# The first chunk of a two-layer kernel is loaded in two halves, the shared weights are loaded ahead of chunk two, and all instruction orders are planned anew

## The chip, the core and the metric

The kernel runs on one core of one Trainium2 chip. The metric is the time of one execution on the device, in microseconds (us); lower is better. Beside each time stands one execution that the hardware profiler recorded; the views below are of that one. The engines are PE (TensorE), DVE (VectorE), ACT (ScalarE), POOL (GpSimd) and SP (SyncE, which here only issues transfers). PEld is PE's loading of stationary operands, which overlaps PE.

## What is computed

A sequence x of 16 batches of 256 rows of 128 features goes through two gated layers; everything is float32. Cut to what matters here:

```python
xn = layernorm(x)                       # 4096 rows of 128
f = xn @ W.T + b                        # layer 0, attention
a = softmax(f @ f.T + distance_bias) @ f      # per batch of 256 rows
shared = (silu(xn @ Gs.T) * (xn @ Us.T)) @ Ds.T          # inner width 256
probs = sigmoid(xn @ router.T + bias)                    # 8 experts
w = top-2 of probs, normalised
combined = sum over the 2 experts of w * ((silu(xn @ G[e].T) * (xn @ U[e].T)) @ D[e].T)
x = x + a * silu(shared + combined)

xn = layernorm(x)                       # layer 1
s = attention over 16 heads, linear in the rows: projection, squares, softmax over heads, output projection
expert of a batch = argmax of a small network on the batch's last row
g = xn + 0.3 * ((gelu(xn @ W1[e] + b1) @ W2[e] + b2) @ Wo + bo)
x = x + s * silu(g)
```

## The kernel before

The 4096 rows are 32 tiles of 128 rows, four to a **chunk** (chunks 0 to 7), two to a batch. There are no loops over engines' work at run time and no scheduler in the compiler's sense: each engine's program is a long list of calls written out by a planner, such as `gate(3, 0)` (step 3, PSUM bank 0), and each step waits on semaphores for what it needs. An engine works through its list strictly in order. So the list decides both what an engine does next and what it waits for next, and a step that waits holds up all that stands behind it on its engine. 71 products of one 128-row unit with one expert (**units** 0 to 70) stand in the middle of the kernel.

The stages, and the lines of the profile that belong to them:

- **Start.** SP issues the loads of x (`load_x`, 256 KB a chunk, L245), of the constants C in three parts (L249, the second part at L257, the third at L264), of WA (router and layer-0 projection, L251) and of WB (the shared expert's weights, L253). PE runs `warm`, products of ones into a bank that nobody reads (L461), until its first real work is there. DVE makes a chunk's moments (`stats0`, L1089 and L1092, waits for the chunk's load), ACT the root (`root0`, L1894), DVE the normalised chunk XA (`norm0`, L1097 and L1100).
- **Layer 0, dense part.** PE turns a chunk (`turn_in`, L474), ACT copies it out as XT (L1907). From XT, PE makes `features` (L484, evicted by DVE at L1119), `gate` (L510) and `up` (L516) of the shared expert, `down` (L524); `turn_f` (L501) turns the features for the scores. DVE's `upper()` (L1124) makes a bf16 copy of a triangle of ones from the second part of C, and waits for its load. `prob`, `best`, `second` (from L1162) choose the two experts of a row, `ranks` on PE (L494) counts, and `positions` on DVE (L1202 to L1222) gives each row its place in a scratch. This is done in two sets: set 0 is chunks 0 to 2, set 1 the rest.
- **Dispatch.** POOL scatters the rows of a tile with two indirect transfers (L2412), 24 transfers for set 0 and 40 for set 1. Meanwhile scores (L532), softmax and `mix` (L551) run.
- **Units.** SP fetches the 128 rows of a unit back from the scratch (`fetch`, L283), PE turns four units at once (`turn_x`, L566), `gate_up` (L580), ACT silu (L1961), DVE `hidden` (L1317), PE `down_e` (L588), ACT scales the result (YS, L1968, eight buffers) and POOL scatters it (`scat`, L2435). A fetch of unit u waits for the scatter of unit u-16. `collect` (L293) loads a chunk's results back, 512 KB each; `root1` (L1894) is the root of the second layernorm.
- **Layer 1.** For chunks 0 to 5 it is begun between the last units, and ends with `store` (L333).

ACT holds the tables of few functions at once: between a root and a silu stands an ACT_TABLE_LOAD.

Of the kernel before, what the change touches and what calls it, by code (L numbers as in the profile page):

```python
# [34 lines left out]
WARM = 32  # L35
# [35 lines left out]
def program(nc, D, out):  # L71
    with ExitStack() as ctx:
# [88 lines left out]
        d_x = [sem(f"d_x{c}") for c in range(8)]  # L161
        d_id, d_wa, d_c, d_di, d_fill, d_dist = (sem("d_" + n) for n in ("id", "wa", "c", "di", "fill", "dist"))
# [75 lines left out]
        ident = c_("ident")  # L238
# [4 lines left out]
        def _(e):  # L243
# [105 lines left out]
            fetch(5)  # L349
            ends()  # L350
            fetch(6)
# [19 lines left out]
            store_b()  # L371
            fetch(26)
            fetch(27)
            load_w2()
# [3 lines left out]
            fetch(31)  # L378
            fetch(32)
# [6 lines left out]
            fetch(39)  # L386
            fetch(40)
# [7 lines left out]
            collect(1)  # L395
            fetch(47)
            fetch(48)
            collect(2)
            fetch(49)
            fetch(50)  # L400
            fetch(51)
            fetch(52)
# [15 lines left out]
            fetch(68)  # L418
            collect(3)
            collect(4)  # L420
            collect(5)
            store_w2(0)
            fetch(69)
            fetch(70)
            store_w2(1)
# [17 lines left out]
            expert1(13)  # L443
            expert1(14)
            store(0)
            expert1(15)
            store(1)
# [9 lines left out]
        def _(e):  # L457
# [9 lines left out]

            def turn_in(c, k, free=None, n=0):
                e.wait_ge(s_xa, c + 1)
                if c == 0:  # L470
                    e.wait_ge(d_id, 16)
                when(free, n)
                for j in range(4):
                    m = e.transpose(PS[k][:, j * 128:(j + 1) * 128], XA[:, 4 * c + j, 0:128], ident)  # L474
                m.then_inc(p_xt, 1)

            def features(b, k, free=None, n=0):

                e.wait_ge(s_xt, b // 2 + 1)
# [24 lines left out]
            def gate(j, k, free=None, n=0):  # L504
                c, f = divmod(j, 2)
                e.wait_ge(s_xt, c + 1)
                if j == 0:
                    e.wait_ge(d_wb, 16)
                when(free, n)
# [189 lines left out]
            turn_in(0, 0)  # L699
            gate(0, 0)  # L700
            features(0, 6)
            gate(1, 2)
            features(1, 3)
            turn_in(1, 0, s_sg, 1)
            up(0, 5)
            features(2, 0)
            up(1, 1)
            features(3, 3, s_f, 2)
            turn_in(2, 2, s_sg, 2)
            turn_f(0, 4)  # L710
            gate(2, 7)
            features(4, 3, s_f, 4)
            features(5, 2)
            up(2, 6)
            gate(3, 0)
            gate(4, 5)
            turn_in(3, 1, s_hh, 2)
            up(3, 2)
            down(0, 4, s_ft, 1)
            features(6, 1)  # L720
            ranks(0, 7, s_sg, 3)
            gate(5, 3)
            up(4, 1, s_f, 7)
            gate(6, 5, s_sg, 5)
            gate(7, 0)
            up(5, 7, s_places, 1)
            down(1, 6)
            turn_in(4, 2)
            up(6, 1)
            gate(8, 5)  # L730
            turn_f(1, 3)
            turn_f(2, 2)
            features(7, 4)
            down(2, 7)
            up(7, 3, s_ft, 2)
            turn_in(5, 6)
            gate(9, 4, s_f, 8)
            features(8, 0)
            features(9, 6, s_xt, 6)
            turn_in(6, 5)  # L740
            features(10, 1, s_hh, 7)
            features(11, 2)
            features(12, 0, s_f, 9)
            gate(10, 7)
            turn_in(7, 2, s_f, 12)
            up(8, 4, s_sg, 10)
            features(13, 3)
# [335 lines left out]
        def _(e):  # L1083
# [19 lines left out]
            def stats0(c):  # L1103
                e.wait_ge(d_x[c], 16)
                moments(4 * c, 4, s_mv)
# [1513 lines left out]
```

## Time and profile before

| | us |
|---|---|
| median of 3 runs | 285.37 (283.64 to 285.94) |
| the profiled execution's own time | 284.54 |
| its span on the core | 282.7 |

The profiled execution's own time is 1.8 us over its span: that much lies around the part that the engines' records cover. The page of the profile gives busy time of each engine, the same in 40 slices, and the costliest groups; the timeline gives single instructions with the idle time of their engine just before them and what released it.

### The profile page before, as it was taken

The numbers are of one execution on the slowest core, as the hardware profiler recorded it, in microseconds if no ns is written. First come the engines' busy times: TensorE is split into PE (matmuls) and PEld (weight loads), VectorE is DVE, ScalarE is ACT, GpSimd is POOL, SyncE is SP. The second block draws the span as 40 slices with busy tenths as digits, with TensorE's granted clock in tenths as the row PEclk, the third lists the DMA queues.
The fourth block names the chain that finished last, engine by engine and source line by source line (L and its number), as shares of the span: only waits on it lengthen the run. The fifth ranks groups of instructions, "written<-read, shape, count | busy, mean of one in ns | idle before, by whom it ended". The sixth has DMA issues, their size and how long they took to land.

```text
span 282.7 us, 6870 instructions
## 1 busy us (share of the span) xinstructions
PE 267.5 (95%) x1982; PEld 231.1 (82%) x1982; DVE 220.4 (78%) x828; ACT 192.4 (68%) x443; POOL 155.5 (55%) x175
## 2 busy tenths in 40 slices
PE   8899999999999999999999899999998989989992
PEld 5566877667898999999899899999887668858892
DVE  4898987996668668545455579858989999998996
ACT  2876764434555586466455466869979989989882
POOL 3100777777777777777677563773644853121140
PEclk9999999999999999999999999999999999999999
DMA  6997111113562111236432742234613847501813
GB/s 194 313 401 257 47 51 57 49 57 85 144 147 65 47 59 56 78 114 218 132 95 77 255 140 67 76 96 150 210 56 106 183 150 225 135 20 46 264 65 114
DMA packets 31221, 36.03 MB, mean 127 GB/s; under 512 B 4792, under 2 KB 24386, under 8 KB 30928
## 3 DMA queue, kind: packets, MB, share of 16 engines
q1 hardware_dynamic: 26864, 27.13, 32.8%
q0 software_dynamic: 4320, 8.47, 8.9%
q8 instruction: 17, 0.28, 0.4%
q14 instruction: 20, 0.16, 0.2%
HBM read 22.97 MB, written 14.12 MB: 131 GB/s over the span
## 4 chain that ended last, share of the span: by engine, by line
PE 59%; DVE 13%; DMA 9%; issue 8%; POOL 4%; ACT 3%; SPq 2%; DVEq 1%; POOLq 0%; ACTq 0%
PE PS L580 13%; PE PS L588 7%; PE PS L551 5%; PE PS L524 5%; PE PS L532 5%; PE PS L516 5%; PE PS L510 4%; DMA yc_scratch<-YS,XS 3%; POOL yc_scratch L2435 2%; PE PS L484 2%; DMA DI<-in_dest 2%; PE PS L566 2%; DMA XB<-yc_scratch 2%; DMA XB<-wf_scratch 2%; PE PS L666 1%
## 5 line engine op out<-in xcount | busy, mean ns | idle before, releaser
L2435 POOL DMA_INDIRECT yc_scratch<-YS,XS x71 | 73.3, 1032 | 40.8 <-ACT YS L1968 25.5
L580 PE MATMUL PS<-XG,XT 128*128 128x128 f32 x568 | 71.8, 276 | 0.6 <-DVE HHE L1317 0.5
L580 PEld LDWEIGHTS PS<-XG,XT 128*128 128x128 f32 x568 | 67.3, 192 | 1.7 <-issue 1.4
L1317 DVE TENSOR_TENSOR HHE<-EP,PS 128x256 f32<-128x256 f32 x71 | 28.6, 415 | 25.0 <-ACT EP L1961 17.6
L2412 POOL DMA_INDIRECT xs_scratch<-XA,POS x32 | 31.8, 994 | 22.9 <-issue 22.9
L1961 ACT ACTIVATE EP<-PS 128x256 f32<-128x256 f32 x71 | 26.6, 388 | 24.4 <-PE PS L580 21.9
L588 PE MATMUL PS<-WE,HHE 128*128 x284 | 41.2, 279 | 1.2 <-DVE HHE L1317 1.0
L588 PEld LDWEIGHTS PS<-WE,HHE 128*128 128x128 f32 x284 | 36.2, 191 | 3.5 <-issue 3.3
L2412 POOL DMA_INDIRECT xs_scratch<-XB,POS x32 | 31.6, 989 | 9.8 <-issue 9.8
L1329 DVE COPY XT<-WE 128x512 f32 x71 | 29.9, 443 | 5.6 <-PE PS L580 5.3
L1968 ACT ACTIVATE YS<-PS,XS 128x128 f32<-128x128 f32 x71 | 25.3, 371 | 9.0 <-PE PS L588 8.4
L2421 POOL COPY XT<-C 128x256 f32<-128x256 f32 x16 | 5.9, 400 | 24.8 <-DVE C L1438 24.7
L1100 DVE TENSOR_SCALAR XA<-X,MV,RS 128x128 f32<-128x128 f32 x64 | 19.1, 375 | 0.6
L551 PE MATMUL PS<-F,EP 128*128 128x129 f32 x128 | 16.9, 277 | 0.6 <-ACT EP L1937 0.5
L510 PE MATMUL PS<-XT,WB 128*128 128x512 f32 x32 | 16.3, 601 | 0.9 <-DMA WB<-in_wb 0.9
L551 PEld LDWEIGHTS PS<-F,EP 128*128 128x128 f32 x128 | 15.6, 191 | 1.8 <-ACT EP L1937 0.9
L524 PEld LDWEIGHTS PS<-WB,EP 128*128 128x128 f32 x128 | 15.2, 192 | 1.9 <-issue 1.2
L1089 DVE BATCH_NORM_STATS2 ST<-X 128x6 f32<-128x128 f32 x64 | 13.8, 276 | 3.7 <-DMA X<-in_x 3.7
L532 PE MATMUL PS<-FT 128*128 128x256 f32 x64 | 16.2, 381 | 0.0
L516 PE MATMUL PS<-XT,WB 128*128 128x512 f32 x32 | 16.2, 593 | 0.0
L1298 DVE CUSTOM_DVE_ANT_0 EP<-PS,C 128x256 f32<-128x256 f32 x32 | 12.2, 420 | 5.0 <-ACT EP L1937 3.6
L1937 ACT ACTIVATE EP<-EP 128x512 f32<-128x512 f32 x16 | 10.0, 629 | 8.9 <-DVE EP L1306 5.0
(222 smaller groups left out, 562.1 us busy)
## 6 DMA issues: line engine op xcount, KB each, us to landing
XS<-xs_scratch SPq DMA_DIRECT2D x71, 65.0 KB
XB<-yc_scratch SPq DMA_DIRECT2D x8, 512.0 KB, 4.6
WE<-in_we SPq DMA_DIRECT2D x1, 3072.0 KB, 14.7
X<-in_x SPq DMA_DIRECT2D x8, 256.0 KB, 5.6
out<-X SPq DMA_DIRECT2D x8, 256.0 KB, 2.5
S<-wf_scratch SPq DMA_DIRECT2D x7, 257.0 KB, 3.8
XB<-wf_scratch SPq DMA_DIRECT2D x6, 257.0 KB, 4.0
yc_scratch<-YS,XS POOLq DMA_INDIRECT x71, 2.4
```

The source lines that it names most:

```text
L510: e.matmul(PS[k][:, :], WB[:, f * 128:(f + 1) * 128], tile(XT, 4 * c, 4), start=True, stop=True).then_inc(p_g, 1)
L516: e.matmul(PS[k][:, :], WB[:, 256 + f * 128:256 + (f + 1) * 128], tile(XT, 4 * c, 4), start=True, stop=True).then_inc(p_u, 1)
L524: m = e.matmul(PS[k][:, t * 128:(t + 1) * 128], HHS[:, (2 * c + f) % 3, t * 128:(t + 1) * 128], WB[:, 512 + f * 128:512 + (f + 1) * 128], ...
L532: m = e.matmul(PS[k][:, i * 256:(i + 1) * 256], tile(FT, 2 * b + i), tile(FT, 2 * b, 2), start=True, stop=True)
L551: m = e.matmul(PS[k][:, i * 129:(i + 1) * 129], PT[:, kb, j, i * 128:(i + 1) * 128], F[:, 2 * b + j, 0:129], start=j == 0, stop=j == 1)
L580: m = e.matmul(PS[k][:, f * 128:(f + 1) * 128], WC[:, u % 4, f * 128:(f + 1) * 128], XG[:, g % 2, j * 128:(j + 1) * 128], start=True, stop ...
L588: m = e.matmul(PS[k][:, 0:128], HHE[:, u % 3, f * 128:(f + 1) * 128], WE[:, bass.ds(reg[u // 4][u % 4] + (512 + f * 128), 128)], start=f = ...
L1317: e.tensor_tensor(HHE[:, u % 3, :], SGE[:, u % 3, :], PS[k][:, 256:512], ALU.mult).then_inc(s_hhe, 1)
L1329: e.tensor_copy(WC[:, u % 4, :], WE[:, bass.ds(reg[u // 4][u % 4], 512)]).then_inc(s_wc, 1)
L1961: e.activation(SGE[:, u % 3, :], PS[k][:, 0:256], ACT.Silu, bias=0.0, scale=1.0).then_inc(s_sge, 1)
L2412: e.indirect_dma_start(out=xs, out_offset=bass.IndirectOffsetOnAxis(ap=POS[:, s, t:t + 1], axis=0), in_=T[:, t, :], in_offset=None, bounds ...
L2435: e.indirect_dma_start(out=yc, out_offset=bass.IndirectOffsetOnAxis(ap=XS[:, g % 4, j, 128:129].bitcast(U32), axis=0), in_=YS[:, u % 8, :] ...
```

## The change

1. Chunk 0 is loaded, normalised, turned and copied in two halves of 128 KB (`load_half`, `stats_first`, `norm_first`, `turn_first`, `root_first`); the first product with WB goes in two halves too, so that its first half needs only the first half of the chunk. The semaphores of the following chunks count one more.
2. WB is issued as SP's fourth load, ahead of chunk 1, no longer behind chunk 2.
3. `warm` makes 18 products instead of 32.
4. The lists of PE, DVE, ACT, SP and POOL and the PSUM banks of all steps are planned anew.

```diff
-WARM = 32
+WARM = 18
...
-            load_x(0)
+            def load_half(b):
+                e.dma_start(X[:, 2 * b:2 * b + 2, :].rearrange("p i d -> p (i d)"),
+                            D["x"].rearrange("(c b) (p i) d -> c b p (i d)", b=2, i=2)[0, b]).then_inc(d_x[0] if b else d_xh, 16)
+
+            load_half(0)
             e.dma_start(C[:, 0:129], D["consts"][:, 0:129]).then_inc(d_id, 16)
+            load_half(1)
+            e.dma_start(WB[:, :], D["wb"]).then_inc(d_wb, 16)
             load_x(1)
             e.dma_start(WA[:, :], D["wa"]).then_inc(d_wa, 16)
             load_x(2)
-            e.dma_start(WB[:, :], D["wb"]).then_inc(d_wb, 16)
...
             def gate(j, k, free=None, n=0):
                 c, f = divmod(j, 2)
-                e.wait_ge(s_xt, c + 1)
                 if j == 0:
+                    e.wait_ge(s_xt, 1)
                     e.wait_ge(d_wb, 16)
+                    when(free, n)
+                    e.matmul(PS[k][:, 0:256], WB[:, 0:128], tile(XT, 0, 2), start=True, stop=True)
+                    e.wait_ge(s_xt, 2)
+                    e.matmul(PS[k][:, 256:512], WB[:, 0:128], tile(XT, 2, 2), start=True, stop=True).then_inc(p_g, 1)
+                    return
+                e.wait_ge(s_xt, c + 2)
...
+            def stats_first():
+                e.wait_ge(d_xh, 16)
+                moments(0, 2, s_mv)
+
+            def norm_first():
+                e.wait_ge(s_sd, 1)
+                normalize(0, 2, s_xa)
...
+            stats_first()
             stats0(0)
+            norm_first()
             norm0(0)
             stats0(1)
+            upper()
             stats0(2)
             norm0(1)
+            features(0, 1)
+            norm0(2)
```

The orders as built, at the three places that matter below. **DVE at the start, before**, from the end of chunk 2's moments (BN_AGGR) to the CAST of `upper()`; RECIPROCAL and TENSOR_SCALAR are a chunk's normalisation:

```order
L1092 BN_AGGR MV<-ST 128x2 x4
L1097 RECIPROCAL RS<-RS 128x4
L1100 TENSOR_SCALAR XA<-X,MV,RS 128x128 x4
L1128 COPY XA<-DI 128x32
L1129 COPY XB<-DI 128x32
L1119 TENSOR_TENSOR F<-PS,WA 128x274
L1089 BN_STATS ST<-X 128x6 x4
L1092 BN_AGGR MV<-ST 128x2 x4
L1119 TENSOR_TENSOR F<-PS,WA 128x274
L1097 RECIPROCAL RS<-RS 128x4
L1100 TENSOR_SCALAR XA<-X,MV,RS 128x128 x4
L1124 CAST BFC<-C 128x128
```

**DVE at the start, after**, from the moments of chunk 1, which stand behind both halves of chunk 0:

```order
L1108 BN_STATS ST<-X 128x6 x4
L1111 BN_AGGR MV<-ST 128x2 x4
L1151 CAST BFC<-C 128x128
L1108 BN_STATS ST<-X 128x6 x4
L1111 BN_AGGR MV<-ST 128x2 x4
L1116 RECIPROCAL RS<-RS 128x4
L1119 TENSOR_SCALAR XA<-X,MV,RS 128x128 x4
L1146 TENSOR_TENSOR F<-PS,WA 128x274
L1116 RECIPROCAL RS<-RS 128x4
L1119 TENSOR_SCALAR XA<-X,MV,RS 128x128 x4
L1146 TENSOR_TENSOR F<-PS,WA 128x274
L1155 COPY XA<-DI 128x32
```

The CAST of `upper()`, which waits for the second part of C, has moved from behind the normalisations of chunks 1 and 2 to a place ahead of the moments of chunk 2, and so ahead of both; the copies from DI have moved behind them.

**SP at the start, before**, where each row is one load:

```order
L245 DMA X<-in_x 128x2x256
L249 DMA C<-in_consts 128x129
L245 DMA X<-in_x 128x2x256
L251 DMA WA<-in_wa 128x274
L245 DMA X<-in_x 128x2x256
L253 DMA WB<-in_wb 128x768
L245 DMA X<-in_x 128x2x256 x2
L257 DMA C<-in_consts 128x258
L258 DMA DI<-in_dest 128x64
```

**SP at the start, after**:

```order
L250 DMA X<-in_x 128x256
L254 DMA C<-in_consts 128x129
L250 DMA X<-in_x 128x256
L256 DMA WB<-in_wb 128x768
L246 DMA X<-in_x 128x2x256
L258 DMA WA<-in_wa 128x274
L246 DMA X<-in_x 128x2x256 x3
L263 DMA C<-in_consts 128x258
```

The load of WB has moved ahead of those of chunk 1, WA and chunk 2. The bytes ahead of the second part of C (the 128x258 row) are the same as before.

**SP in the middle, before**, from the table load ahead of unit 44 (L283 is a fetch, L293 a collect; an ISA row sets up the fetch behind it):

```order
L231 TENSOR_LOAD EI
L283 ISA
L283 DMA XS<-xs_scratch 128x130
L293 DMA XB<-yc_scratch 128x2x512
L283 ISA
L283 DMA XS<-xs_scratch 128x130
L283 ISA
L283 DMA XS<-xs_scratch 128x130
L293 DMA XB<-yc_scratch 128x2x512
L283 ISA
L283 DMA XS<-xs_scratch 128x130
L231 TENSOR_LOAD EI
```

**SP in the middle, after**, at the same place:

```order
L232 TENSOR_LOAD EI
L289 ISA
L289 DMA XS<-xs_scratch 128x130
L299 DMA XB<-yc_scratch 128x2x512
L289 ISA
L289 DMA XS<-xs_scratch 128x130
L289 ISA
L289 DMA XS<-xs_scratch 128x130
L289 ISA
L289 DMA XS<-xs_scratch 128x130
L232 TENSOR_LOAD EI
L289 ISA
```

The collect of chunk 0 still stands behind the fetch of unit 44, but that of chunk 1 no longer stands between the fetches of units 46 and 47; it and the next come behind unit 51.

Two more moves, read off the lists by hand: the `turn_x` of units 28 to 31 stands behind 1.8 us more of PE's work than before, and that of units 44 to 47 behind 1.3 us more (each step counted at the time that its products took before); and on ACT `root1` of chunks 0, 1 and 2 stands in one run between one pair of ACT_TABLE_LOADs, where chunk 2 had its own pair before. ACT has 33 such loads where it had 35.

## Rows read from the trace of the kernel before

**Rows 1.** The page: busy time of all engines, then PE, DVE and POOL in 40 slices (tenths).

```profile
PE 267.5 (95%) x1982; PEld 231.1 (82%) x1982; DVE 220.4 (78%) x828; ACT 192.4 (68%) x443; POOL 155.5 (55%) x175
...
PE   8899999999999999999999899999998989989992
```

**Rows 2.** Windows: stretch, its length, busy (and instructions) of PE, PEld, DVE, ACT, POOL, clock, DMA.

```profile
2.00:6.00 4.00, 4.00 (x21) 2.82 (x20) 2.09 (x12) 0.53 (x3) 0.40 (x2) 1.00 0.85 265
6.20:7.00 0.80, 0.80 (x9) 0.72 (x8) 0.80 (x5) 0.00 (x0) 0.49 (x1) 1.00 1.10 294
28.00:40.00 12.00, 12.00 (x83) 9.66 (x82) 11.79 (x54) 9.09 (x17) 9.26 (x10) 1.00 0.15 50
140.00:180.00 40.00, 38.19 (x327) 36.85 (x327) 27.10 (x78) 24.21 (x62) 24.58 (x24) 1.00 0.40 120
180.00:220.00 40.00, 38.06 (x324) 35.22 (x324) 33.21 (x122) 34.89 (x87) 22.48 (x22) 1.00 0.39 124
220.00:240.00 20.00, 18.92 (x132) 14.22 (x132) 18.95 (x82) 18.91 (x47) 11.16 (x16) 1.00 0.66 180
```

**Rows 3.** Timeline of the first 14 us: start, length, engine, line, tiles, count, idle before.

```profile
1.32 6.02 PE L461 MATMUL PS<-BFC 128*128 128x256 bf16 x32 [1.32 <-POOL ONE L2386]
...
3.51 0.87 DVE L1089 BATCH_NORM_STATS2 ST<-X 128x6 f32<-128x128 f32 x4 [3.51 <-DMA X<-in_x]
...
4.72 0.47 SPq L257 DMA_DIRECT2D C<-in_consts  x1
...
7.18 0.60 PE L474 MATMUL PS<-C,XA 128*128 128x128 f32 x4
...
7.63 0.87 DVE L1089 BATCH_NORM_STATS2 ST<-X 128x6 f32<-128x128 f32 x4 [0.22 <-DMA X<-in_x]
...
8.69 1.10 PE L510 MATMUL PS<-XT,WB 128*128 128x512 f32 x2 [0.90 <-DMA WB<-in_wb]
...
8.88 1.11 DVE L1100 TENSOR_SCALAR XA<-X,MV,RS 128x128 f32<-128x128 f32 x4
...
11.41 0.60 PE L474 MATMUL PS<-C,XA 128*128 128x128 f32 x4
...
13.67 0.22 DVE L1124 CAST BFC<-C 128x128 bf16<-128x128 f32 x1
```

**Rows 4.** DMA issues of the first 16 us: KB each, median us from issue to landing.

```profile
WB<-in_wb SPq DMA_DIRECT2D x1, 384.0 KB, 5.3
...
C<-in_consts SPq DMA_DIRECT2D x1, 129.0 KB, 5.6
```

**Rows 5.** Timeline of DVE: `best(0)` begins, and `positions(0)` begins.

```profile
18.91 0.31 DVE L1162 TENSOR_REDUCE RW<-XS 128x12 f32<-128x96 f32 x1
...
24.44 0.34 DVE L1202 TENSOR_TENSOR_SCAN XS<-ONE,PS 128x96 f32<-128x96 f32 x1
```

**Rows 6.** Timeline of POOL: the first dispatch, and the end of its unbroken work.

```profile
27.88 1.15 POOL L2412 DMA_INDIRECT xs_scratch<-XA,POS  x1 [13.45 <-issue]
...
141.51 0.97 POOL L2435 DMA_INDIRECT yc_scratch<-YS,XS  x1 [0.88 <-ACT YS L1968]
```

**Rows 7.** Timeline of PE, 120 to 215 us: three of the rows with idle time.

```profile
137.43 0.66 PE L566 MATMUL PS<-C,XS 128*128 128x128 f32 x4 [0.54 <-DMA XS<-xs_scratch]
...
161.19 0.66 PE L566 MATMUL PS<-C,XS 128*128 128x128 f32 x4 [0.92 <-DMA XS<-xs_scratch]
...
199.19 1.16 PE L688 MATMUL PS<-WD,XA 128*128 128x128 f32 x8 [0.51 <-DVE HHE L1317]
```

**Rows 8.** Timeline of SP's queue around the first collects.

```profile
156.32 0.43 SPq L293 DMA_DIRECT2D XB<-yc_scratch  x1
156.99 2.65 SPq L283 DMA_DIRECT2D XS<-xs_scratch  x2
```

**Rows 9.** Timeline of ACT around the root of chunk 2 in layer 1.

```profile
190.91 1.28 ACT L1894 ACT_TABLE_LOAD   x1
...
193.26 1.28 ACT L1961 ACT_TABLE_LOAD   x1
```

More of the change, by code:

```diff
@@ new lines, in _ @@
+            features(3, 7)
+            turn_f(0, 6)
+            features(4, 4, s_f, 3)
+            features(5, 0)
+            gate(3, 1, s_hh, 2)
+            turn_f(1, 0, s_f, 6)
+            down(0, 7)
+            turn_in(3, 4)
+            up(2, 5)
+            turn_f(2, 3, s_sg, 3)
+            gate(4, 2)
+            up(3, 0, s_ft, 2)
+            features(6, 4)
+            ranks(0, 2, s_sg, 5)
+            up(4, 1)
+            gate(5, 7, s_sh, 1)
+            features(7, 6)
+            up(5, 5, s_hh, 3)
@@ new lines, in _ @@
+            gate(6, 7, s_sg, 6)
+            gate(7, 0, s_hh, 4)
+            down(1, 3)
+            up(6, 6, s_f, 8)
+            up(7, 7, s_sg, 7)
+            turn_in(4, 3, s_sh, 2)
+            turn_f(3, 1)
+            down(2, 0, s_sg, 8)
+            gate(8, 5)
+            up(8, 1, s_ft, 4)
+            gate(9, 6, s_hh, 7)
+            features(8, 3)
+            turn_in(5, 4)
+            features(9, 5, s_sg, 9)
+            up(9, 7)
+            turn_in(6, 3, s_f, 9)
+            features(10, 4)
@@ L2217, in _ @@
-            gate(42, 2)
-            down_e(39, 0)
-            fuse(0, 5)
-            down_e(40, 3)
+            down_e(29, 0)
+            down_e(30, 2)
+            gate(31, 1)
+            gate(32, 6)
+            gate(33, 4)
+            turn_x(9, 7)
+            down_e(31, 0)
+            down_e(32, 7)
+            gate(34, 2)
+            gate(35, 4)
+            down_e(33, 0)
+            gate(36, 1)
+            gate(37, 7)
+            down_e(34, 5)
+            down_e(35, 6)
+            gate(38, 4)
@@ new lines, in _ @@
+            turn_x(10, 3)
+            gate(39, 7)
+            down_e(36, 4)
+            down_e(37, 0)
+            down_e(38, 7)
+            gate(40, 6)
+            turn_x(11, 4)
+            gate(41, 1)
+            gate(42, 2)
+            down_e(39, 1)
+            gate(43, 0)
+            down_e(40, 4)
+            gated(0)
+            down_e(41, 1)
+            turn_x(12, 4)
+            down_e(42, 7)
+            down_e(43, 1)
+            gate(44, 6)
+            gate(45, 0)
+            gate(46, 7)
@@ L2272, in _ @@
+            gate(58, 5)
+            turn1(1, 6)
+            down_e(55, 0)
+            keep(0, 4)
+            squares(1, 0)
+            down_e(56, 2)
+            turn1(2, 6)
+            gate(59, 7)
+            keep(1, 0)
+            gate(60, 5)
             down_e(57, 4)
@@ L2291, in _ @@
+            heads(0, 5)
+            turn_x(16, 1)
+            squares(2, 3)
+            gate(63, 0)
+            down_e(59, 2)
+            keep(2, 3)
+            down_e(60, 6)
+            gated(4)
+            gate(64, 1)
+            down_e(61, 0)
+            fuse(2, 5)
+            fuse(3, 6)
+            gate(65, 7)
+            gated(5)
+            turn_x(17, 3)
+            gate(66, 4)
+            down_e(62, 0)
             sel_exp(0)
-            down_e(62, 4)
             down_e(63, 0)
-            fuse(2, 3)
```

1680 lines of the change are left out of this document (803 added, 877 removed).

## The prediction

> **What bounds the kernel now.** I read the page's busy times first: PE is busy 267.5 us of a 282.7 us span, DVE 78%, ACT 68%, POOL 55% [rows 1]. The slices show where PE is not full: the first two, and the last third. The windows say the same in us [rows 2]. From 28 to 40 PE has no idle time at all and DVE hardly any (11.79 of 12.00), and PE's slices stay full from there to the last third. From 140 to 220 PE idles 3.75 us in short waits, and from 220 on DVE and ACT are as full as PE (18.95 and 18.91 of 20). So a microsecond lost or won ahead of 28 us has nothing behind it that soaks it up until about 137 us; and behind 220 us the end is set by DVE's fixed work. I compared what stands on DVE behind the last unit's `hidden` in both lists: the same steps, but for their order. The end moves as that point moves.
>
> Then the start, in the timeline [rows 3]. Idle products run from 1.32 to 7.34. DVE gets chunk 0 at 3.51. PE's first real product is at 7.18, and it stops once for WB: 0.90 us, until 8.69. Chunk 1 is normalised from 8.88 to 9.99, PE turns it at 11.41. POOL's first dispatch is at 27.88, and then it works without a gap that matters until it first waits a long time for ACT, 0.88 us ahead of 141.51 [rows 6].
>
> **The change, part by part.**
>
> *Halves, and fewer idle products.* The first half of chunk 0 is half the bytes; I put its landing at 3.1 us (the whole lands at 3.51, rows 3; landing is mostly a fixed time, so I give the half only 0.4 us). Two moments instead of four (0.45 us), but the second half's moments stand between it and its normalisation, so both are done at about 4.7, and the first half's normalisation ends near 5.5, the second's near 6.2. The 18 products end near 5.2: some 19 fit into the 4 us from 2 to 6 [rows 2], 0.21 us each, and they begin at 1.32. PE thus turns the first half at 5.6 instead of 7.18: **1.6 us earlier**. The split itself costs nothing on PE (2 + 2 turns, 256 + 256 columns), and on ACT one fixed cost more of about 0.3 us, beside idle time.
>
> *WB earlier.* WB was issued sixth and landed 5.3 us later [rows 4], about 8.5, with 969 KB of other loads ahead (by the sizes of the tiles); now 320 KB stand ahead. It lands near 6, and the wait of 0.90 goes. But chunk 1's load now ends where 960 KB have landed, near 7.5 (chunk 2's did, and was waited for until 7.63, rows 3), and chunk 2's where WB's did, about 8.5. By itself that is cheap: by PE's own times the products on chunk 0 (one `gate`, two `features`, a `gate`, an `up`) last 3.9 us, to about 10.
>
> *The copy of the triangle.* Here the new order has a price that the diff does not show. `upper()` needs the second part of C. That load was issued at 4.72 [rows 3] and took 5.6 us to land [rows 4]: 10.3. The bytes ahead of it are the same now, so it still lands at 10.3 or a little later. Before, DVE came to it at 13.67 and waited for nothing. Now it stands ahead of chunk 2's moments and chunk 1's normalisation, and DVE's list is strict. DVE has chunk 1's moments done near 8.8, **waits until 10.35**, copies (0.22), makes chunk 2's moments (1.1, as from 7.63 to the reciprocal at 8.70) and normalises chunk 1 (1.3, from there to 9.99): done at 12.9 instead of 9.99. PE is out of work at about 10, waits nearly 3 us, and turns chunk 1 at 13.0 instead of 11.41. Behind it on DVE stand the evictions of `features`, chunk 2 (ready at 14.6, was 13.75) and chunk 3.
>
> Following these steps on with the durations of the trace, the last of set 0's features is evicted at about 19.4, then comes chunk 3's normalisation, and `best(0)` begins at 20.7 instead of 18.91. One `up` (0.68) stands between it and `positions(0)`, but before, DVE waited there for PE anyway, so `positions(0)` begins near 26.0 instead of 24.44 [rows 5], and the first dispatch is at **29.4 instead of 27.88**. PE reaches `ranks(0)` 1.7 us later than before, with 0.9 us more of other work done: it is **0.9 us behind**. With DVE full from 28 to 40 and 1.5 us behind, PE's lag grows a little: I take 1.1 us. Bounds: 0.9 us ahead, if the part of C lands by the time chunk 2 does (PE then keeps the one extra product of 0.86 us that it has done when it turns chunk 1); 2.0 behind, if all of DVE's lag becomes PE's.
>
> *The middle.* PE waited 0.54 us at 137.43 and 0.92 at 161.19 for rows of units 28 to 31 and 44 to 47 [rows 7]. The first waits hang on scatters, which POOL, full since the first dispatch, makes at its own pace; it is now 1.5 us later, but PE comes there with 1.8 us more work ahead and 1.1 of lag, so the wait goes. The second followed the collects: that of chunk 1 was issued at 156.32, ahead of the fetch of unit 47 at 156.99 [rows 8]; it now comes behind unit 51, and `turn_x` behind 1.3 us more work. That wait should go too. Together 1.46; since a wait that goes often lets the next step wait for another engine, I count 1.0 (bounds 0 and 1.5).
>
> *ACT's tables.* The root of chunk 2 had a pair of loads of its own, 1.28 us each, at 190.91 and 193.26 [rows 9]. ACT is 87% busy there (34.89 of 40), and PE waited 0.51 us at 199.19 for a `hidden` that waits for ACT's silu. The pair goes; I count 0.3 (bounds 0 and 0.51).
>
> *The rest of the new orders.* PE's steps, units and evictions change places all through, and no row says what that is worth. PE's idle time from 140 to 220 is 3.75 us, of which I have used 0.8 (the other 0.5 lies ahead of 140). I take nothing, with 2 us to either side: twice the longest single wait there (0.92), once gained and once lost. One place at the end is tight: SP issued the last expert's load behind the first store; now it stands behind the second one, but its product has also moved back by 3.3 us of PE's work. Nothing, then.
>
> **The sum.** 284.54 + 1.1 - 1.0 - 0.3 = 284.3 us. The profiled execution lay 0.83 under the median of the three and 0.90 over the lowest; for a median I add a third of the 0.83 and forecast **284.6**.
>
> **Rivals.**
>
> *A. DVE's wait is carried in full (slower).* Chunk 1 is 2.9 us late at 12.9, and each later microsecond in the landing of C's part adds one. DVE is full until 40 us and its list is strict, so the lag can stay near 2 to 2.9 instead of melting to 1.1, in PE's work as well. Then the units come late too, and only half of the middle's 1.3 is won back: 284.54 + 2.5 - 0.65 = 286.4, up to 288.5 if the new orders lose as well. It decides from a lag of 1.3 us on, what the middle gives. For it: 11.79 of 12.00 [rows 2]. Against it: at the start PE and ACT still have short idle times in which 1 us can be made up, as my walk through them shows.
>
> *B. The clock.* While it was fed idle products PE came to its higher level (2.4 GHz) late: 21 instructions touch the 4 us from 2 to 6, nine the 0.8 us from 6.2 to 7.0, twice the rate; the clock column reads 1.00 in both [rows 2]. In the new order PE stands idle around 5.3 and then from 10 to 13. No row has so long a gap so early. If the lower level (1.2 GHz) came back for as long as it lasted at first, 4.9 us, half of the work of that time is lost: 2.4 us at most, and part of it lies in PE's waits for DVE. 284.6 + 1.5 = 286.1, at most 287.0.
>
> The Trainium skill ("TensorE: Matmul & The Clock Gate", Part 1) says that the gate falls back to half rate once the engine has been idle for long, and warns of waits for DMA between short bursts of products; by that rule rival B would come true if the wait for chunk 1 is long enough. No run here shows yet whether it does; I weigh it low, since PE's 0.90 us wait at 7.8 left the clock up.
>
> *C. The order pays in full (faster).* The wait for C is short (the load lands near 9), PE keeps its lead of 0.9, both waits and the table pair go and nothing takes their place: 284.54 - 0.9 - 1.46 - 0.51 = 281.7.
>
> *D. Nothing arrives.* The lag and what is won in the middle are both absorbed by DVE's work behind 220 us: 284.5, the same as before.
>
> **How the numbers follow.** The forecast with its neighbours (283.0 to 286.2) has 0.45, D 0.12, A 0.16, B 0.08, C 0.19. From 281.5 to 287.6 these leave out about 0.1 on either side. About 1% of the time, 2.9 us, is what a measurement tells from no change: under 282.5 lie C and a small part of the rest (0.2), over 288.2 the worse half of A with some of B (0.13), the remainder is the same (0.67).
>
> **What would show it.** In the profile after: the CAST of `upper()` at 10.3 to 10.7 with DVE idle ahead of it and released by the load of C; the normalisation of chunk 1 ending near 12.9; PE idle for over 2 us ahead of turning chunk 1; the first dispatch near 29.4; no wait for XS near units 28 and 44. I am wrong if the CAST finds its data there, if PE turns chunk 1 before 11.4, if the first dispatch is no later than 27.9, or if the middle has new waits of over 2 us together.

## The result, and the profile after

| | us |
|---|---|
| before, median of 4 runs beside them | 284.50 (283.57 to 285.94) |
| after, median of 4 runs | 289.24 (287.56 to 291.93) |
| ratio | 1.0147, 95% interval 1.0101 to 1.0193 |
| the profiled execution of after: its time, its span | 289.94, 288.1 |

The changed kernel is slower by 1.5%: 4.2 us by the ratio, 5.4 us by the profiled executions. The forecast was 284.6 with a range from 281.5 to 287.6. One of the four runs after (291.93) was in a slower state of the chip, and the ratios, here and below, leave such runs out. So what an edit saves is given below as the difference of two ratios times 284.5 us, with the 95% intervals of both put together.

The page of the profile after: busy time, PE in 40 slices, and the granted clock in the same slices.

```profile
PE 269.1 (93%) x1970; PEld 234.6 (81%) x1970; DVE 222.5 (77%) x829; ACT 190.0 (66%) x443; POOL 156.9 (54%) x175
...
PE   7599999999995999999999999999999878999993
...
PEclk9979999999999599999999999999999999999999
```

Against [rows 1] PE has two dents, in the second slice and in the thirteenth, and PEclk a dent behind each of them. The clock of before had none. Fewer instructions (1970, not 1982) take more busy time (269.1, not 267.5). Some of them ran at the lower level of the clock (1.2 GHz, half of the higher one): from 15 to 18 us and from 90 to 100 us the granted clock was 0.57 and 0.66 (windows below).

The timeline after, first 32 us: start, length, engine, line, tiles, count, idle before.

```profile
1.32 4.02 PE L467 MATMUL PS<-BFC 128*128 128x256 bf16 x18 [1.32 <-POOL ONE L2425]
...
5.50 0.66 PE L479 MATMUL PS<-C,XA 128*128 128x128 f32 x2 [0.16 <-DVE XA L1119]
...
9.71 1.02 PE L534 MATMUL PS<-XT,WB 128*128 128x512 f32 x2
11.46 0.23 DVE L1151 CAST BFC<-C 128x128 bf16<-128x128 f32 x1 [3.89 <-DMA C<-in_consts]
...
12.85 1.12 DVE L1119 TENSOR_SCALAR XA<-X,MV,RS 128x128 f32<-128x128 f32 x4
...
14.02 1.05 PE L486 MATMUL PS<-C,XA 128*128 128x128 f32 x4 [3.29 <-DVE XA L1119]
...
14.86 1.91 PE L534 MATMUL PS<-XT,WB 128*128 128x512 f32 x2
...
31.40 1.15 POOL L2451 DMA_INDIRECT xs_scratch<-XA,POS  x1 [15.17 <-issue]
```

Read it beside [rows 3] and [rows 6]. PE has its first tiles at 5.50, 1.7 us earlier. Then DVE stands 3.89 us at the CAST, because the second part of C is not there; chunk 1 is normalised at 13.97 (9.99 before), PE waits 3.29 us and turns it at 14.02 (11.41). What it does then runs at half rate: two products of 512 columns take 1.91 us at 14.86 and 1.02 at 9.71. The first dispatch is at 31.40, 3.5 us later.

The second dent. First PE, then the sync engine's queue of the same stretch, then the copy of the unit table.

```profile
89.24 1.06 PE L569 MATMUL PS<-F,EP 128*128 128x129 f32 x8
93.72 1.12 PE L584 MATMUL PS<-C,XS 128*128 128x128 f32 x4 [3.42 <-DMA XS<-xs_scratch]
94.63 1.92 PE L550 MATMUL PS<-FT 128*128 128x256 f32 x4
...
78.67 3.94 SPq L289 DMA_DIRECT2D XS<-xs_scratch  x7
83.11 7.55 SPq L347 DMA_DIRECT2D xs_scratch<-YS  x8
90.87 4.14 SPq L289 DMA_DIRECT2D XS<-xs_scratch  x7
...
77.64 0.26 DVE L1313 CAST EI<-PS 2x128 int32<-2x128 f32 x1
```

L584 is `turn_x(1)`, which turns the rows of units 4 to 7 and so needs the fetch of unit 7. That fetch was issued at 90.87, behind `ends()`: eight stores at the ends of the experts' rows, 7.55 us of the queue. They could not begin sooner, because the queue stood at the fetch of unit 0, which waits for the unit table, copied at 77.64. The same things in the trace of before, sync queue, DVE, PE:

```profile
67.29 3.29 SPq L283 DMA_DIRECT2D XS<-xs_scratch  x6
71.16 6.13 SPq L341 DMA_DIRECT2D xs_scratch<-YS  x8
77.90 4.26 SPq L283 DMA_DIRECT2D XS<-xs_scratch  x7
...
66.15 0.28 DVE L1286 CAST EI<-PS 2x128 int32<-2x128 f32 x1 [0.34 <-PE PS L560]
...
99.78 0.60 PE L566 MATMUL PS<-C,XS 128*128 128x128 f32 x4
```

The stores stood among the fetches there too, but the table was copied 11.5 us earlier, and PE came to this step only at 99.78, not at 90.3. The new orders moved the table back and the step ahead, and the two met. (Of the 11.5 us, 3.6 are the late start's: with the CAST moved back, run 1 below, the table is copied at 74.06.)

Windows of the trace after, with the columns of [rows 2].

```profile
12.00:15.00 3.00, 0.98 (x5) 0.98 (x6) 2.93 (x17) 2.18 (x3) 0.62 (x1) 0.86 1.32 260
15.00:18.00 3.00, 3.00 (x12) 1.93 (x11) 2.68 (x15) 2.67 (x4) 0.61 (x1) 0.57 0.96 380
28.00:40.00 12.00, 12.00 (x61) 7.92 (x61) 11.62 (x57) 8.29 (x14) 6.77 (x7) 1.00 0.10 35
90.00:100.00 10.00, 6.58 (x31) 5.92 (x30) 3.38 (x15) 2.69 (x9) 7.56 (x9) 0.66 0.50 124
...
140.00:180.00 40.00, 39.66 (x350) 39.20 (x349) 25.35 (x68) 21.94 (x62) 27.61 (x28) 1.00 0.54 161
180.00:220.00 40.00, 39.89 (x338) 37.55 (x336) 36.12 (x131) 34.61 (x88) 22.55 (x22) 1.00 0.39 121
220.00:240.00 20.00, 16.35 (x125) 12.23 (x125) 18.35 (x85) 18.12 (x47) 11.33 (x16) 1.00 0.56 157
```

From 90 to 100 PE is busy 6.58 us at a granted clock of 0.66. From 140 to 220 it idles 0.45 us, where it idled 3.75 before [rows 2]. From 220 to 240 it idles 3.65 instead of 1.08, so of the 3.3 us less in the first stretch 2.6 come back in the second.

Where the end hangs can be read from the 71 `hidden` steps: shortest, median and longest in ns, then the starts of the first and the last. Before, after, and run 3 below:

```profile
L1317 DVE TENSOR_TENSOR HHE<-EP,PS x71: 381/420/423, 103.3 to 217.0; 128x256 f32<-128x256 f32 x71
...
L1344 DVE TENSOR_TENSOR HHE<-EP,PS x71: 385/416/423, 110.2 to 221.5; 128x256 f32<-128x256 f32 x71
...
L1344 DVE TENSOR_TENSOR HHE<-EP,PS x71: 386/417/423, 100.9 to 212.7; 128x256 f32<-128x256 f32 x71
```

From the last one to the end of the span it is 65.7 us before and 66.6 after: of the 5.4 us between the spans, 4.5 are there at the last `hidden`.

### The profile page after: what moved, and what is told of

Same layout as the page of the kernel before. It is cut to its first block, busy times and chain, and to the rows that moved or that the text cites. A ratio compares the mean times of both kernels' runs of the same rounds, so it can differ in the third digit from the quotient of the medians.

```text
span 288.1 us, 6848 instructions
## 1 busy us (share of the span) xinstructions
PE 269.1 (93%) x1970; PEld 234.6 (81%) x1970; DVE 222.5 (77%) x829; ACT 190.0 (66%) x443; POOL 156.9 (54%) x175
## 4 chain that ended last, share of the span: by engine, by line
PE 72%; DVE 10%; SPq 5%; DMA 5%; issue 4%; POOL 2%; ACT 1%; DVEq 0%; POOLq 0%
PE PS L598 22%; PE PS L606 11%; PE PS L542 5%; PE PS L534 5%; PE PS L528 4%; PE PS L569 3%; PE PS L550 3%; PE PS L584 3%; PE PS L496 2%; PE PS L684 2%; DMA C<-in_consts 2%; PE PS L695 2%; PE PS L627 2%; SPq L347 1%; DMA XB<-wf_scratch 1%
## 5 line engine op out<-in xcount | busy, mean ns | idle before, releaser
L606 PE MATMUL PS<-WE,HHE 128*128 x284 | 40.6, 278 | 0.5 <-DVE HHE L1344 0.5
L1356 DVE COPY XT<-WE 128x512 f32 x71 | 30.7, 448 | 7.0 <-PE PS L598 3.5
L2460 POOL COPY XT<-C 128x256 f32<-128x256 f32 x16 | 6.8, 455 | 23.9 <-DVE C L1465 23.6
L1119 DVE TENSOR_SCALAR XA<-X,MV,RS 128x128 f32<-128x128 f32 x64 | 18.0, 359 | 0.6
L569 PE MATMUL PS<-F,EP 128*128 128x129 f32 x128 | 17.6, 287 | 0.0
L534 PE MATMUL PS<-XT,WB 128*128 128x512 f32 x32 | 17.0, 626 | 0.0
L569 PEld LDWEIGHTS PS<-F,EP 128*128 128x128 f32 x128 | 16.8, 205 | 0.2
L550 PE MATMUL PS<-FT 128*128 128x256 f32 x64 | 16.9, 396 | 0.0
L542 PE MATMUL PS<-WB,EP 128*128 128x128 f32 x128 | 15.6, 275 | 0.0
```

Source lines behind the costliest of these rows:

```text
L534: e.matmul(PS[k][:, :], WB[:, 256 + f * 128:256 + (f + 1) * 128], tile(XT, 4 * c, 4), start=True, stop=True).then_inc(p_u, 1)
L542: m = e.matmul(PS[k][:, t * 128:(t + 1) * 128], HHS[:, (2 * c + f) % 3, t * 128:(t + 1) * 128], WB[:, 512 + f * 128:512 + (f + 1) * 128], ...
L550: m = e.matmul(PS[k][:, i * 256:(i + 1) * 256], tile(FT, 2 * b + i), tile(FT, 2 * b, 2), start=True, stop=True)
L569: m = e.matmul(PS[k][:, i * 129:(i + 1) * 129], PT[:, kb, j, i * 128:(i + 1) * 128], F[:, 2 * b + j, 0:129], start=j == 0, stop=j == 1)
L606: m = e.matmul(PS[k][:, 0:128], HHE[:, u % 3, f * 128:(f + 1) * 128], WE[:, bass.ds(reg[u // 4][u % 4] + (512 + f * 128), 128)], start=f = ...
L1356: e.tensor_copy(WC[:, u % 4, :], WE[:, bass.ds(reg[u // 4][u % 4], 512)]).then_inc(s_wc, 1)
```

## The experiments

Two theories. **A**: the CAST's wait for the constants makes the start late and drops the clock. **B**: the fetch of unit 7 behind the stores stops PE and drops the clock again. Their rivals: the delay is taken up by later slack; POOL's chain or the tail of the new orders is what decides; or only the clock counts. Times below are medians on the device; before measured 284.71 in the first group, 284.41 in the second, 284.99 in the third.

**1. The CAST back (a_upper).**

```diff
             stats0(1)
-            upper()
             stats0(2)
...
             features(1, 2)
+            upper()
             slots()
```

> Changed kernel with one step moved back: VectorE takes the CAST of the second part of the constants after features(1), just ahead of the slots, and no longer between the statistics of chunk 1 and those of chunk 2; all other orders stay. Theory A (the early CAST is what makes chunk 1 late and lets TensorE's clock fall at 14.1 us): chunk 1 is normalised near 10 us instead of 12.85, the 3.3 us wait ahead of turning it goes to under 1 us, no half clock before 20 us, the first dispatch moves from 31.4 to 28 or 29, and the time falls by 2.5 to 3.5 us from 289.2 to near 286.2, since the later wait for rows of XS moves along and stays. Rival (the start is absorbed by what comes later, the wait for XS or the GpSimd chain): the first dispatch moves but the time stays within 1 us of 289.

Measured: 285.45, ratio to before 1.0039 (1.0006 to 1.0072), so 3.1 us under the changed kernel, 1.6 to either side. Its timeline:

```profile
11.66 0.66 PE L486 MATMUL PS<-C,XA 128*128 128x128 f32 x4 [1.28 <-DVE XA L1119]
...
27.83 1.15 POOL L2451 DMA_INDIRECT xs_scratch<-XA,POS  x1 [13.96 <-issue]
...
89.25 0.66 PE L584 MATMUL PS<-C,XS 128*128 128x128 f32 x4 [2.54 <-DMA XS<-xs_scratch]
```

The first dispatch is where it was before the change, 3.6 us earlier than in the changed kernel, and the saving at the end is of that size. Not all of it need be the start's: the wait for XS shrank by 0.9 to 2.54 us, and its products ran at full rate. Theory A holds; that later slack absorbs it falls.

**2. The stores first (a_ends).**

```diff
             copy_w1()
+            ends()
             fetch(0)
...
             fetch(6)
-            ends()
             fetch(7)
```

> Changed kernel with one step moved on the sync engine's queue: the eight stores at the experts' ends go ahead of the first fetch, where that queue has nothing to do until the unit table is there, and no longer between the fetches of units 6 and 7. Theory B (fetch 7 stood behind those stores for 7.5 us and TensorE waited 3.4 us for it, after which its clock was half for 6.8 us): the wait ahead of turn_x(1) goes to 0, the half clock from 92.7 to 99.5 us goes with it, and the time falls by 3.4 us of waiting and up to 3.4 us of half clock, from 289.2 to 283 to 285. Rival (GpSimd's row stores and the fetches behind them set the pace of the middle, so that what is saved at 90 us is waited for at 100 to 240 us): 288 to 289. A second rival (the stores delay the first fetches, since the unit table comes soon): the wait moves to turn_x(0).

Measured: 283.89, ratio 0.9959 (0.9922 to 0.9997), 5.3 us under the changed kernel, 1.7 to either side. The stores and fetches of its sync queue, and PE's two waits:

```profile
61.83 6.11 SPq L347 DMA_DIRECT2D xs_scratch<-YS  x8
78.38 10.80 SPq L289 DMA_DIRECT2D XS<-xs_scratch  x16
...
13.93 0.66 PE L486 MATMUL PS<-C,XA 128*128 128x128 f32 x4 [3.54 <-DVE XA L1119]
...
90.05 0.60 PE L584 MATMUL PS<-C,XS 128*128 128x128 f32 x4
```

The stores fit into time in which the queue stood idle, `turn_x(1)` no longer waits, and the first wait is still there in full. Theory B holds. What is saved at 90 us arrives at the end, so neither POOL nor the fetches took it up: the first dispatch is at 31.32 here, as late as in the changed kernel, and the kernel is still 0.4% under the one before.

**3. Both (a_both).** The two edits together.

> Changed kernel with both steps moved: the CAST of the constants back behind features(1), the eight stores at the experts' ends ahead of the first fetch. If the two waits with their falls of the clock are the whole loss, the savings add up (3 and 5 us) and the time is near 281.5, below the kernel before (284.5), and what the new orders give in the middle shows. If something in the tail (the waits from 220 to 240 us) takes part of it, 283 to 285. If neither wait mattered, 289.

Measured: 281.19, ratio 0.9861 (0.9812 to 0.9910). The savings are 3.1 and 5.3 us alone and 8.1 together (1.9 to either side). With the stores already first, the CAST's place costs 2.8 us (run 2 against this one, 1.8 to either side). PE's granted clock in slices, and its longest waits:

```profile
PEclk9999999999999999999999999999999979999999
...
PE PS L663 <- DVE FT L1487: 2.1, 1, 2.1
PE PS L633 <- DVE RB L1429: 1.7, 2, 1.1
```

Two misplaced steps cost 8 us, and hid that the rest of the change is worth 4.0 us (1.4%). The last `hidden` begins at 212.7, 4.3 us earlier than before, but from there to the end of the span it is 68.5 us where it was 65.7: the new tail gives a part back (11).

**4. The clock alone (a_warm).** All steps as in the changed kernel, with idle products in the two waits.

```diff
+            warm(28)
             turn_in(1, 6)
...
+            warm(30, 5)
             turn_x(1, 5)
```

> Changed kernel with idle products added on TensorE in its two long waits (28 ahead of turning chunk 1, 30 ahead of turn_x(1), 256 columns each, into the bank that the turn then overwrites); no step is moved, so both waits for data stay. It tells the clock from the waits. If the falls of the clock to half after each wait cost time (half of 3.4 us and half of 6.8 us of products), the clock stays full and the time falls by about 5 us to 284 or so. If only the waits count, because the half speed is taken up by later slack, 288 to 289.5. If the idle products run longer than the waits, 290 or more.

Measured: 285.57, ratio 1.0046 (1.0012 to 1.0080), 2.9 us under the changed kernel (1.6 to either side), by work that computes nothing. The first filling and the step behind it, the second, and the first dispatch:

```profile
10.16 3.22 PE L467 MATMUL PS<-BFC 128*128 128x256 bf16 x28
13.21 0.60 PE L486 MATMUL PS<-C,XA 128*128 128x128 f32 x4
...
87.68 3.44 PE L467 MATMUL PS<-BFC 128*128 128x256 bf16 x30
90.95 0.60 PE L584 MATMUL PS<-C,XS 128*128 128x128 f32 x4
...
28.95 1.15 POOL L2453 DMA_INDIRECT xs_scratch<-XA,POS  x1 [13.84 <-issue]
```

Both turns take 0.60 us instead of 1.05 and 1.12, and PEclk is 9 in every slice. So of the 8 us about 2.9 are the clock's and the rest is waiting. In this profile the second part of C landed 1.1 us sooner than in the changed kernel's (CAST at 10.35); how much of the 2.9 is such chance the runs don't tell. The first dispatch is 2.45 us earlier: 1.1 for the landing leave some 1.3 for the half rate at the start.

**5. The transfer instead of the step (c_early).** The second part of C is issued behind WA, ahead of chunk 2; the CAST stays.

```diff
             e.dma_start(WA[:, :], D["wa"]).then_inc(d_wa, 16)
+            lo = CW["dist"][0]
+            e.dma_start(C[:, 129:lo], D["consts"][:, 129:lo]).then_inc(d_c, 16)
             load_x(2)
             for c in range(3, 5):
                 load_x(c)
-            lo = CW["dist"][0]
-            e.dma_start(C[:, 129:lo], D["consts"][:, 129:lo]).then_inc(d_c, 16)
```

> Changed kernel with the transfer moved instead of the step: the second part of the constants (129 KB) is issued right behind WA, ahead of chunk 2, and the CAST stays where the change put it; the stores at the experts' ends stay behind fetch 6. Theory A says that the CAST is late because its transfer lands at 11.4 us: then it lands near 9, the CAST no longer stops VectorE, chunk 1 is turned by 11.5, the first dispatch comes at 28 to 29, and the time falls by 3 to 4 us to near 285.5, as it did when the step was moved (285.45). Rival (the landing is set by all that is in flight, so that an earlier place gains little, or chunk 2 lands as much later and VectorE waits there): the first dispatch stays above 30 and the time within 1.5 us of 289.

The first round of this kernel and of the next three fell on a stretch in which every kernel on the chip, the one before too (379.0 us), stood still for about 95 us; it gives only the first 30 us, and each was run again. (That round: 383.1 us; no ratio can be given.)

> The kernel of c_early once more (second part of the constants issued ahead of chunk 2, CAST where the change put it), since all engines, in the kernel before too, stood still for some 90 us from 38 us on in the first round of it. Its first 30 us were as theory A has it: CAST at 7.8 us, chunk 1 turned at 11.4, first dispatch at 27.4. So the time should be 3.5 to 4 us under that of the changed kernel, 285.2 to 286; the rival's 288 to 289 would now mean that a start 4 us earlier does not last.

Measured: 285.43, ratio 1.0034 (0.9998 to 1.0070): 3.2 us saved, as much as moving the step gave. Its timeline:

```profile
8.45 0.23 DVE L1151 CAST BFC<-C 128x128 bf16<-128x128 f32 x1 [0.86 <-DMA C<-in_consts]
...
11.63 0.66 PE L486 MATMUL PS<-C,XA 128*128 128x128 f32 x4 [1.20 <-DVE XA L1119]
```

It was the landing, then, and not DVE's time for the CAST.

**6. The same misplacing in the kernel before (b_upper).**

```diff
             stats0(1)
+            upper()
             stats0(2)
...
             norm0(2)
-            upper()
```

> Kernel before with one line moved: the CAST of the constants between the statistics of chunk 1 and those of chunk 2, as in the changed kernel, all else as before. The part landed at 10.3 us there. If that place alone is what costs, chunk 1 is turned near 12.9 instead of 11.4 us, the first dispatch comes 1.5 us later and the time rises by 1.5 to 2 us to near 286.3; with a fall of the clock in the wait 3 us, 287.7. Rival (this kernel has slack there, since WB and the products of chunk 0 come later): within 0.7 us of 284.7.

> The kernel of b_upper once more (kernel before with the CAST between the statistics of chunk 1 and of chunk 2). Its first 30 us had the CAST at 10.3, chunk 1 turned at 12.8 (11.4 before) and the first dispatch at 30.0 (27.9 before). The time should rise by 1.5 to 2.5 us to 286 to 287; rival: slack takes it up, within 0.7 us of before.

First round: ratio 1.0079 (1.0025 to 1.0133) between times that both hold the standstill. Second: 286.69, ratio 1.0072 (1.0043 to 1.0101): 2.0 us slower, 0.8 to either side. Timeline of the second (its profiled execution, 290.30, was the longest of its ten, so only the start is compared):

```profile
10.61 0.23 DVE L1124 CAST BFC<-C 128x128 bf16<-128x128 f32 x1 [3.03 <-DMA C<-in_consts]
...
13.16 0.66 PE L474 MATMUL PS<-C,XA 128*128 128x128 f32 x4 [1.31 <-DVE XA L1100]
```

DVE stands 3.03 us, PE 1.31, and PE's clock stays up there. The same place costs 2.0 us here and 2.8 to 3.1 in the changed kernel, where PE, done sooner with chunk 0, stood 3.3 us and lost its clock. The intervals are too wide to show that the second is dearer.

**7. What the halves are worth (both_nohalf).** In the best version chunk 0 is again one transfer; the steps for its halves both wait for it.

```diff
-            load_half(0)
+            load_x(0)
...
-            load_half(1)
...
-                e.wait_ge(d_xh, 16)
+                e.wait_ge(d_x[0], 16)
```

> The best version so far (281.2 us: CAST moved back, stores at the ends first) with chunk 0 again in one transfer of 256 KB; the steps for its two halves stay as they are, both wait for the whole. It measures what the halves are worth. If the start of TensorE sets the time, turning the first tiles moves from 5.5 to about 6.8 us and the time rises by 1 to 1.5 us to 282.5. Rival (chunk 1 and the first dispatch are set by the landing of chunk 1 and of the constants, so that the early half gains nothing that lasts): within 0.5 us of 281.2, or below it, since one issue less stands ahead of the others.

> The kernel of both_nohalf once more (best version, chunk 0 in one transfer). In its first 30 us the first turn stood at 5.46 us and the first dispatch at 27.3, no later than in the best version (6.18 and 28.3). So the halves should be worth nothing that can be measured: 280.5 to 282. A rise by 1 us or more to 282.5 would show that they do count.

First round: ratio 0.9975 (0.9933 to 1.0017) between times that both hold the standstill. Second: 281.85, ratio 0.9892 (0.9828 to 0.9956), which can't be told from the 0.9861 with halves: 0.9 us slower, 2.3 to either side. PE turns the first tiles at 5.62 here and at 6.18 in a_both: the second half there landed late enough to hold DVE until 4.64. So it is not the halves that make the first product early. They are worth nothing that these runs can measure, but four runs of each don't rule out the 1 to 1.5 us that were expected.

**8. What the early WB is worth (both_wblate).** In the best version WB is issued behind chunk 2.

```diff
-            e.dma_start(WB[:, :], D["wb"]).then_inc(d_wb, 16)
             load_x(1)
             e.dma_start(WA[:, :], D["wa"]).then_inc(d_wa, 16)
             load_x(2)
+            e.dma_start(WB[:, :], D["wb"]).then_inc(d_wb, 16)
```

> The best version so far (281.2 us) with the shared weights WB issued behind chunk 2, as in the kernel before. It measures what their early issue is worth. TensorE's gate(0) stands right behind the two turns and waits for WB; if WB then lands near 8 instead of 6 us, gate(0) and all behind it move by 1.5 to 2 us and the time rises to near 283, a little less since WA, chunk 1 and chunk 2 come sooner. Rival (VectorE sets the first dispatch, and it does not need WB): within 0.5 us of 281.2, with the first dispatch no later than 28.3.

> The kernel of both_wblate once more (best version, WB issued behind chunk 2). In its first 30 us gate(0) waited 2.3 us for WB to 8.78, the clock fell to half for a while, and the first dispatch came at 29.8 (28.3). The time should rise by 1.5 to 2.5 us to near 283.2; rival: within 0.5 us of 281.2.

First round: ratio 1.0001 (0.9957 to 1.0045) between times that both hold the standstill. Second: 284.16, ratio 0.9977 (0.9940 to 1.0014), 3.3 us over a_both, 1.7 to either side. Its clock in slices and its timeline:

```profile
PEclk9599999999999999999999999999999999999999
...
8.66 1.19 PE L522 MATMUL PS<-XT,WB 128*128 128x256 f32 x2 [1.96 <-DMA WB<-in_wb]
...
30.77 1.15 POOL L2451 DMA_INDIRECT xs_scratch<-XA,POS  x1 [16.75 <-issue]
```

With these orders, WB late means a wait of 1.96 us, half rate in the second slice and a first dispatch 2.4 us later. The 3.3 us are most of the 4.0 that the best version is ahead of the kernel before. But they hold the half rate too, which need not come with a late WB: the kernel before waited 0.90 us for WB and its clock stayed up. No run has WB late and the clock up in the new orders, so the load's own worth stays open.

**9. What the fewer idle products are worth (best_w32).** The best version with `WARM = 32`.

> The best version so far (281.2 us: CAST back, stores at the ends first) with 32 idle products at the start instead of 18, as in the kernel before; it undoes the one part of the change that no run has undone. 18 of them ended at 5.34 us and TensorE then waited up to 0.8 us for the first tiles; 32 end at 6.3. The forecast (fewer idle products are free and give room to an early first product) says up to 1 us slower, 282. Rival (products at full clock from 6 us on make up for it, and VectorE sets chunk 1 anyway): within 0.5 us of 281.2, or faster.

Measured: 281.37, ratio 0.9877 (0.9838 to 0.9917): no difference from a_both that shows (0.5 us, 1.8 to either side). PE's first tiles are turned at 7.36 in its profile, but the products behind them run at full rate at once (0.70 us for the first two with WB at 8.21, 1.22 in a_both), and PE turns chunk 1 at 11.83 (12.61 in a_both). The rival held.

**10. Both cures of the CAST (best_cearly).** The best version with the edit of 5.

> The best version so far (281.2 us) with the second part of the constants issued ahead of chunk 2 as well. If the CAST was all that this part held up, nothing is left to gain once the CAST stands behind features(1): 281 to 281.7. Rival (chunk 2 lands 0.5 us later and VectorE waits for it): 0.5 us slower, 281.9.

Measured: 281.79, ratio 0.9894 (0.9858 to 0.9929). Nothing is gained; whether it is the 281 to 281.7 of its first line or the rival's 281.9, the interval does not say.

**11. The tail's clock (best_tail).** As best_cearly, with idle products in the wait near 223 us.

```diff
             heads(4, 5)
+            e.wait_ge(s_ot, 1)
+            warm(14, 7)
             spread(3, 4, s_ot, 2)
```

> As best_cearly, with 14 idle products in the 2.1 us wait near 223 us (behind the first attn_out, into the bank it has read), so that TensorE does not stand idle there. If the fall of the clock after that wait (half for 3.4 us in the profiles) costs its half, and VectorE does not set the tail, the clock stays full and the time falls by up to 1.7 us against best_cearly. Rival (VectorE, busy 18.3 of 20 us from 220 to 240, sets the tail, so the half clock is hidden): the clock stays full and the time within 0.5 us of best_cearly.

Measured: 281.20, ratio 0.9880 (0.9838 to 0.9923), 0.6 us under best_cearly, less than the intervals tell apart. The window from 220 to 240 us of best_cearly:

```profile
220.00:240.00 20.00, 17.75 (x115) 15.32 (x114) 18.24 (x77) 16.67 (x33) 8.60 (x11) 0.91 0.45 136
```

and of best_tail:

```profile
220.00:240.00 20.00, 18.52 (x140) 15.75 (x133) 19.35 (x84) 17.29 (x35) 9.68 (x12) 1.00 0.48 135
```

The clock stays up and DVE gets more done (19.35 us of 20, not 18.24). In the profiles, the time from the last `hidden` to the end of the span is 68.6 us in best_cearly (from 211.8 to 280.4) and 66.7 in best_tail (212.7 to 279.4), 1.9 less. So, by these profiles, most of what the new tail gives back (3) is its clock's. Why the medians show only a third of the 1.9 is not settled; best_tail's own profile had its first tiles late (6.50) and its clock fell at the start.

## Why the prediction was wrong, point by point

- **First product, 1.6 us earlier: right.** 5.50 for a forecast of 5.6. But no worth of it shows: with 32 idle products PE turns its first tiles at 7.36, and the time is the same (9).
- **The CAST waits, and chunk 1 is late: right in its mechanism, mis-sized.** I put the landing at 10.35; it came at 11.4 in this profile and in a_ends, at 10.35 in a_warm, at 10.6 in b_upper2. So PE turned chunk 1 at 14.02, not 13.0. **The first failed step** is "I take 1.1 us" for what is left of it at the end. This place costs 2.0 us in the kernel before and 2.8 to 3.1 in the changed one (6, 3, 1): rival A's 2.5, a lag that is carried in full, is nearer. `ranks(0)` on PE, forecast 1.7 us later, began at 27.66 instead of 23.88, 3.8 later.
- **First dispatch at 29.4: off by 2 us (31.40).** In a_warm, where the landing was the forecast's and the clock stayed up, `ranks(0)` began at 25.21 and the first dispatch at 28.95. So my walk from step to step through the start was sound; what it lacked is 1.1 us of landing and some 1.3 of half rate (4).
- **Rival B, the clock, "I weigh it low": the second failed step.** The sum has no term for it. It came true twice, at 14 and at 93 us, and is worth about 2.9 us (4). The evidence that I set against it, PE's 0.90 us wait that left the clock up, says nothing on a wait of 3 us. The rule of the Trainium skill ("TensorE: Matmul & The Clock Gate", Part 1) that I quoted spoke for it, and the trace agrees: the granted clock was 0.57 from 15 to 18 us behind the wait of 3.29, and 0.66 from 90 to 100 around the one of 3.42. Shorter waits are another matter (last section).
- **The rest of the new orders, "I take nothing": the third failed step, and the dearest.** The wait for XS at 93.72 is 5.3 us with its clock (2), where I allowed 2 us for everything. I compared waits that stood in the profile before and asked whether they went; I did not follow the steps that had moved ahead to what they would now wait for. The orders showed it: the copy of the unit table moved behind other steps of DVE, `turn_x(1)` moved ahead (87.07 in a_both, 99.78 before, with nearly the same first dispatch), and the eight stores still stood between the fetches of units 6 and 7, the last fetch that this step needs.
- **The middle, -1.0: right in sign, too small.** Both waits for XS [rows 7] are gone. The rest of the change is worth 4.0 us once the two steps are moved, where the terms of the middle and of the tables gave 1.3; 4.3 us are there at the last `hidden`. How the 4.0 part between the middle, the early WB and the tables no run separates.
- **"The end moves as that point moves."** In the changed kernel nearly so (65.7 us from the last `hidden` to the end, then 66.6); in a_both not (68.5), where the clock falls near 225 us.
- **ACT's tables, -0.3.** The pair is gone and so is PE's wait at 199; no run separates it.
- **Rival C, 281.7,** is what the kernel gives once the two steps are moved (281.19 to 281.79). Which of its terms came so is not shown: the early first product is worth nothing that shows (9), a late WB costs 3.3 us together with its half rate (8), and nothing separates the tables from the middle.
- **The ranges do not agree with each other.** I left 0.1 over 287.6 but gave 0.13 to over 288.2, and rival A's own "up to 288.5" lies outside the range. The measured median lies beyond all three.

In the terms of the sum: forecast +1.1 - 1.0 - 0.3, shown +8.1 for the two misplaced steps and -4.0 for the rest, which is the 4.2 us of the ratio within rounding.

## What to carry to other kernels

For each step that a new order moves ahead, look up what it waits for and when that can be there at the earliest: a transfer's landing, or a fetch behind other issues in a queue. A step that is due late but needs a late transfer belongs behind the work that does not need it, and stores that nobody waits for soon belong where their queue is idle. Price a wait of TensorE of some microseconds with the slower clock that may follow it. And when a large change loses, look for the few misplaced steps before giving it up: here two moved steps were worth 8 us and turned a loss of 1.5% into a gain of 1.4%.

## What was not expected of the hardware

- **A fall of the clock follows some waits and not others of like length.** It stayed up through 2.54 us at 89 us in a_upper and 1.31 in b_upper2; it fell behind 3.29, 3.42 and 3.54 us. Yet behind the same 2.1 us wait near 223 to 234 us it fell in a_upper, a_both and best_cearly and not in the changed kernel, a_ends or a_warm. And it fell with a wait of 1.96 us in both_wblate2 (8) and behind one of 1.49 in best_tail, whose clock and wait are these:

```profile
PEclk9799999999999999999999999999999999999998
...
6.50 0.41 PE L479 MATMUL PS<-C,XA 128*128 128x128 f32 x2 [1.49 <-DVE XA L1121]
```

  The length of the wait alone does not tell these apart; what does is open.
- **With 18 idle products the clock at the start is a matter of chance.** The first two products with WB took 1.22 us in a_both, 1.02 in the changed kernel, 0.69 in a_upper, though PE's instructions ahead of them are the same. (The clock column of the windows shows 1.00 there in all three; the durations tell the level.)
- **Landings scatter by 1 us** between executions with the same issues: the CAST, stopped by the second part of C, ran at 10.35 and at 11.46.
- **A standstill of all engines but POOL.** In b_upper's first round PE was busy 2.96 us from 40 to 60, with the granted clock at 0.63. ACT stood for 17.25 us until 56.91, released by nothing that the trace shows; POOL was busy 15.12 of the 20. Its window:

```profile
40.00:60.00 20.00, 2.96 (x6) 1.63 (x6) 2.28 (x7) 0.60 (x1) 15.12 (x17) 0.63 0.16 54
```
